# Re-planning every engine's order with other durations, other delays, other priorities and other buffer choices

## What is computed

```
x = x + full(layernorm(x))          16 heads of 8, every key seen, softmax
x = x + ffn(layernorm(x))           128 -> 512 -> 128, relu
x = x + causal_and_local(layernorm(x))   two attentions with rotary q and k: causal, then a window of 32
x = x + ffn(layernorm(x))
x = x + padded(layernorm(x))        16 heads, 2 kv heads, a window of 32 around each token
x = x + moe(layernorm(x))           8 experts, top 2: silu(y W1) * (y W2), then W3 (352 wide)
x = x + sink(layernorm(x))          8 heads of 16, window 128 and the first 4 keys
x = x + moe(layernorm(x))
```

## Time and profile before

| what | value |
|---|---|
| median of three timed runs | 2377.37 us (2376.93 to 2382.76) |
| profiled execution, span from first to last instruction | 2437.9 us (its own time is not recorded apart from the span) |
| TensorE, matmuls | 2192.9 us busy, 90% |
| TensorE, weight loads | 1242.7 us, 51% |
| VectorE | 1659.9 us, 68% |
| ScalarE | 1423.4 us, 58% |
| GpSimd | 670.1 us, 27% |
| mean granted TensorE clock | 0.978 |

### The profile page before, as it was taken

How to read it: one execution, slowest core, us unless ns; L and a number is a source line. 1 busy time by engine, 2 the same in 40 slices (tenths; PEclk the granted TensorE clock), 3 DMA queues, 4 the chain that set the end, 5 groups by cost and what they waited for, 6 DMA issues and landing times.

```text
span 2437.9 us, 62962 instructions
## 1 busy us (share of the span) xinstructions
PE 2192.9 (90%) x26266; PEld 1242.7 (51%) x26290; DVE 1659.9 (68%) x3679; ACT 1423.4 (58%) x2105; POOL 670.1 (27%) x602
## 2 busy tenths in 40 slices
PE   7888998999999989899999998998988989999887
PEld 3222232232323324424553686565787877867877
DVE  8998888786788776512754466776574858675644
ACT  1367767868787778797678755454424324344322
POOL 3400000020011102321024352422244544424553
PEclk9999999999999999999999999999999989999999
DMA  6601100211130212210231563222554745634665
GB/s 171 227 17 32 42 16 17 57 45 24 28 90 17 56 23 54 79 43 22 59 99 48 156 173 88 77 78 57 154 159 143 219 133 152 197 85 138 199 201 184
DMA packets 160746, 235.23 MB, mean 96 GB/s; under 512 B 21968, under 2 KB 81872, under 8 KB 160208
## 3 DMA queue, kind: packets, MB, share of 16 engines
q1 hardware_dynamic: 145456, 206.81, 30.6%
q0 software_dynamic: 9984, 20.73, 2.5%
q10 hardware_dynamic: 5024, 3.67, 0.6%
HBM read 156.28 MB, written 73.88 MB: 94 GB/s over the span
## 4 chain that ended last, share of the span: by engine, by line
PE 62%; DVE 14%; ACT 12%; issue 6%; another core or an unknown queue 2%; DMA 2%; POOL 1%; SPq 1%; DVEq 0%; POOLq 0%; ACTq 0%
PE PS L1182 14%; ACT PT L1344 9%; PE PS L1231 8%; PE PS L1162 8%; DVE MS L1586 7%; PE PS L1131 6%; PE PS L1248 5%; PE PS L1118 3%; PE PS L1031 2%; PE PS L992 2%; PE PS L1021 2%; PE PS L1111 2%; PE PS L1192 2%; PE PS L1042 1%
## 5 line engine op out<-in xcount | busy, mean ns | idle before, releaser
L1344 ACT ACTIVATE PT<-PS 128x1024 f32<-128x1024 f32 (+5 forms) x1200 | 1013.1, 905 | 389.7 <-PE PS L1162 368.1
L1586 DVE TENSOR_REDUCE MS<-PS 128x2 f32<-128x1024 f32 (+3 forms) x736 | 783.4, 1099 | 217.6 <-PE PS L1131 196.7
L1182 PE MATMUL PS<-PT,VA 128*9 128x512 f32 (+8 forms) x6720 | 564.4, 436 | 19.9 <-ACT PT L1344 17.8
L1162 PE MATMUL PS<-QO,KO 64*64 64x512 bf16 (+6 forms) x6240 | 424.6, 307 | 40.7 <-ACT PT L1344 31.1
L1162 PEld LDWEIGHTS PS<-QO,KO 64*64 64x64 bf16 (+2 forms) x6240 | 179.9, 106 | 286.8 <-ACT PT L1344 177.1
L1131 PE MATMUL PS<-KO,QO 61*64 61x512 bf16 (+2 forms) x3520 | 287.1, 327 | 27.3 <-DVE MS L1586 14.1
L1231 PE MATMUL PS<-SG,WB 128*128 128x128 f32 x2208 | 286.1, 282 | 10.8 <-DMA WB<-in_mW 5.0
L1231 PEld LDWEIGHTS PS<-SG,WB 128*128 128x128 f32 x2208 | 268.6, 197 | 19.4 <-issue 11.8
L1825 POOL DMA_INDIRECT scr_o<-SG,TO x184 | 182.7, 993 | 251.9 <-ACT SG L1379 226.4
L1131 PEld LDWEIGHTS PS<-KO,QO 61*64 61x64 bf16 (+1 forms) x3520 | 128.4, 105 | 230.6 <-DVE MS L1586 126.5
L1182 PEld LDWEIGHTS PS<-PT,VA 128*9 128x9 f32 (+2 forms) x6720 | 126.7, 90 | 185.1 <-issue 109.8
(11 more groups left out here) (182 smaller groups left out, 2503.7 us busy)
## 6 DMA issues: line engine op xcount, KB each, us to landing
WB<-in_mW SPq DMA_DIRECT2D x184, 384.0 KB
PT<-scr_y SPq DMA_DIRECT2D x40, 264.0 KB, 3.4
PT<-scr_o SPq DMA_DIRECT2D x16, 512.0 KB, 5.4
QO<-scr_q_full SPq DMA_DIRECT2D x32, 192.0 KB
KO<-scr_k_full SPq DMA_DIRECT2D x32, 192.0 KB
QO<-scr_q_causal SPq DMA_DIRECT2D x32, 192.0 KB
QO<-scr_q_local SPq DMA_DIRECT2D x32, 192.0 KB
QO<-scr_q_padded SPq DMA_DIRECT2D x32, 192.0 KB
```

The source lines that it names most:

```text
L1162: p = mm(pb[c:c + n, h2, at:at + tn], k[:, k0 + c:k0 + c + n], q[:, t0:t0 + tn], start=not masked, stop=True, skip_group_check=masked)
L1182: p = mm(bank[32 * h:32 * h + D + 1, c0:c0 + tn], va[0:n, :], pt[0:n, plane, at:at + tn], start=s["first"] and j == 0, stop=s["last"] and ...
L1344: e = activation(pt[0:r, 0:n, a:b], ps[0:r, 0:n, a:b], ACT.Exp, scale=s["A"].scale)
L1586: v.tensor_reduce(to, got, AX.X, ALU.max).then_inc(S["top"], 1)
```

## The change

The instructions are the same, but for six more memsets at the start. What changes is the planner and its numbers.

1. Delays: one figure for all (`HOP`, 200 ns after any step) becomes one by engine (`AFTER`).
2. Durations of nearly all steps are given anew, and those of DMAs too: for the operand loads the transfer goes from 1300 ns to 1800, 2900 or 4000 ns.
3. A product (and an `up`, a `down`) had to wait in the plan for the end of the one before it in its chain and 200 ns more; now it needs only that the other one has begun (`order`).
4. Banks are taken by the longest-free one, other buffers by the first free one; before it was the other way round. A ring `CH` of 2 is taken with each chain's bank.
5. All priorities (`LEADS`, `URGENT`, `SHORT`, `SWITCH`, `WORTH`) are other numbers.
6. All eight PSUM banks are cleared at the start, not two, and TensorE waits for all.

```diff
-HOP = 200.0
-LEADS = dict(full=(2075, -1582, 2002, -3166), ..., moe1=(4124, -3793, 2105, 1583), ..., moe2=(3151, -2635, -2559, -3240))
-SHORT = dict(pe=4316.0, act=969.0, dve=1357.0, pool=17578.0, sp=22529.0)
-SWITCH = dict(whole=165.0, quarters=123.0, columns=118.0)
-WORTH = 93219.0
+LEADS = dict(full=(12575, -313, 10581, -2099), ..., moe1=(79534, -5116, -9726, -12501), ..., moe2=(-35552, -42750, -12205, 41501))
+SHORT = dict(pe=2752, act=1132, dve=1343, pool=7914, sp=10511)
+SWITCH = 100
+WORTH = 497318
+AFTER = dict(pe=215, act=165, dve=125, pool=110, sp=60)
...
-        self.held, self.ordered = {} if held is None else held, held is not None
+        self.name, self.ordered = name, ordered
...
+    def room(self, now, besides=(), leaves=0):
+        spare = [p for p in self.parts if self.since(p) <= now and not any(i in besides for i in p)]
+        if len(spare) <= leaves:
+            return None
+        return spare[0] if self.ordered else min(spare, key=self.since)
...
         for name in names.split():
-            self.due(step.signals[name], 1, at)
+            self.due(step.signals[name], 1, at + AFTER[engine])
...
-    RA = Ring("RA", 0, [(5,), (4,), (6,), (7,)], banks)
-    RB = Ring("RB", 0, [(0, 1), (2, 3), (4, 5), (6, 7)], banks)
-    RP = Ring("RP", 0, [(6,), (7,)], banks)
+    RA = Ring("RA", 0, [(5,), (4,), (6,), (7,)], banks, False)
+    RB = Ring("RB", 0, [(i, i + 1) for i in (0, 2, 4, 6)], banks, False)
+    RP, CH = Ring("RP", 0, [(6,), (7,)], banks, False), Ring("CH", 2)
...
-                chain = dict(po=RP, fc=FC) if A.name == "full" else dict(po=RP)
+                chain = dict(po=RP, ch=CH, fc=FC) if A.name == "full" else dict(po=RP, ch=CH)
...
-                    p = add("product", [("pe", 1.667 * w + 6, "product")], dict(v=v_ready, exp=[x["exp"] for x in was], before=products[-1:]),
+                    p = add("product", [("pe", int(1.667 * w) + 17, "product")], dict(v=v_ready, exp=[x["exp"] for x in was]), order=last,
...
-                        dmas=lambda s, n=n: [("q_in%s" % s.use["qo"].i, n, 2000, 1300)])
+                        dmas=lambda s, n=n: [("q_in%s" % s.use["qo"].i, n, 1600, 4000 if not A.tiled else 2900 if A.group == 1 else 1800)])
...
-                s = add("turn_mul", [("pool", 2120, "turn_mul"), ("dve", 1150, "turn_mul2")], dict(src=ready),
+                s = add("turn_mul", [("pool", 2050, "turn_mul"), ("dve", 1430, "turn_mul2")], dict(src=ready),
...
-                s = add("turn_add", [("dve", 940, "turn_add")], dict(a=[got[g]["turn_mul"], got[g]["turn_mul2"]]),
+                s = add("turn_add", [("dve", 1120, "turn_add")], dict(a=[got[g]["turn_mul"], got[g]["turn_mul2"]]),
...
-            for i in (6, 7):
+            for i in range(8):
                 v.memset(RP[i], 0.0).then_inc(S["cleared"], 1)
```

More of the change, by code:

```diff
@@ L97, in has_all @@
     def has_all(self, now):
-        return all(s.at + HOP <= now for signals in self.needs.values() for s in signals) and all(u.i is not None for u in self.within)
+        return all(s.at <= now for s in self.awaits) and all(u.i is not None for u in self.within)
     def room(self, now):
@@ L118, in __init__ @@
         self.count, self.order, self.steps = {}, {e: [] for e in ENGINES}, []
-        self.free, self.ready, self.times = {e: 0.0 for e in ENGINES}, {e: [] for e in ENGINES}, {0.0}
+        self.free, self.ready, self.times = {e: 0 for e in ENGINES}, {e: [] for e in ENGINES}, set()
         self.banks = {}
-        self.look, self.lead, self.coming, self.mode, self.moving = {}, 0.0, {e: 0.0 for e in ENGINES}, "whole", 0.0
+        self.look, self.lead, self.coming, self.mode, self.moving = {}, 0, {e: 0 for e in ENGINES}, "whole", 0
     def given(self, name, value, at):
@@ L156, in urgency @@
             then = step.on[i + 1][0]
-            short = max(self.free[then] - now, 0.0) + self.coming[then] < SHORT[then]
+            short = max(self.free[then] - now, 0) + self.coming[then] < SHORT[then]
         stays = engine == "pe" and step.mode[0] == self.mode
-        return short, step.far + step.lead + WORTH * stays
+        return short, step.far + step.lead + WORTH * stays, -step.index
     def go(self, step, i, now):
@@ L192, in go @@
                 self.due(step.signals["dma"], 16 * n, self.moving + ns)
+        for use in step.ending:
+            use.since = max(s.at for s in use.ends)
     def run(self):
+        uses = {}
+        for i, step in enumerate(self.steps):
+            step.index, step.awaits, step.ending = i, [s for signals in step.needs.values() for s in signals] + [x.begun for x in step.order], []
+            for use in step.use.values():
+                for s in use.ends:
+                    uses.setdefault(s, []).append(use)
+        for step in self.steps:
+            for s in step.signals.values():
+                step.ending += uses.get(s, [])
         self.look_ahead()
@@ L211, in run @@
             for engine in ENGINES:
-                can = [k for k in self.ready[engine] if self.free[engine] <= now and k[2] <= now and (k[1] or k[0].room(now) is not None)]
-                if can:
-                    k = max(can, key=lambda k: self.urgency(k[0], k[1], now))
-                    self.ready[engine].remove(k)
-                    self.go(k[0], k[1], now)
+                if self.free[engine] <= now:
+                    can = [k for k in self.ready[engine] if k[2] <= now and (k[1] or k[0].room(now) is not None)]
+                    if can:
+                        k = max(can, key=lambda k: self.urgency(k[0], k[1], now))
+                        self.ready[engine].remove(k)
+                        self.go(k[0], k[1], now)
         left = [step for step in self.steps if not step.seen] + [k[0] for e in ENGINES for k in self.ready[e]]
```

256 lines of the change are left out of this document (130 added, 126 removed).

## The result

| | before | after |
|---|---|---|
| median, runs taken together on one chip | 2377.15 us (4 runs, 2374.16 to 2382.76) | 2390.44 us (4 runs, 2388.15 to 2392.25) |
| ratio after / before | | 1.005 [1.0032, 1.0068] |
| profiled execution | 2437.9 us span, later 2379.2 (below) | 2387.4 us span, own time 2389.19 |

The change makes the kernel 0.5% slower, by 13 us. The forecast was 2329 us.

What follows compares the result with a forecast made beforehand. TensorE (PE) was taken as the bound, idle for 245.0 us of a 2437.9 us span. Terms -40 - 10 + 0 + 5 + 0 - 5 = -50 us gave span 2388, times 0.9752 2329 us; 8 in 10: 2245 to 2405 us.

Steps and rivals of the forecast that it cites:

- What bounds the kernel now: the scaling: Whole kernel: idle time read in the profiled span of 2437.9 us, the result multiplied by 0.9752 at the end.
- The orders, with true durations: Last third: truer durations in the plan bring its PE idle time to the preceding 720 us's rate, -40 us (0 to -94).
- Products: PE's 592 products: one in six joins another and saves mode switches, -10 us (0 to -70).
- Delays: Handovers between engines: per-engine delays replace 200 ns and take out a cushion of 35 to 75 ns, 0 (0 to +18).
- the rival without a cushion: PE after exponentials: small ACT delays stop PE, +60 us with only 20 of the gains left, 2416 us; chance 0.21.
- Buffers: PT, QO, KO, WB, HM by the first free lose slack, so ACT's exponentials may wait, +5 us (0 to +36).
- Memsets: Start of the kernel: six more on DVE take 3 us, within 3.56 us idle before the input lands, 0 (0 to +1).
- Clock: Last third: with less PE idle time a part of the granted clock comes back, -5 us (-27 to +10).
- The signs that I listed: Profile after: less late idle time, earlier `up` matmuls, more joined products, no 5 us weight wait, exponential waits near 49 us.
- The 5 us wait for the weights: PE's 4.98 us stall for weights until 1953.0 us should go, as `sink` operand loads are priced at 4000 ns.
- Idle from 1680 us on: Last third: PE's idle time was to be under 60 us, as a sign for the main term.
- the wide mix of the first rival: Early batches' experts run beside later attentions, PE everywhere as full as from 1200 to 1440 us, 2257 us; chance 0.20.

Runs made afterwards that it cites:

- before again: The kernel before, unedited, run once more with the profiler: one execution of 2381.04 us, span 2379.2 us.
- experiment 7: Kernel after without the scatters' landing wait, measured GpSimd prices, longest-free buffers, two new sets of priorities: 2516.7 and 2535.31 us; first set on another chip 2357.48 us.
- experiment 4: Four small memsets put before each of the 64 scatters: kernel after 2434.6 us (1.0232), kernel before 2403.68 us (1.0101).
- Experiment 6: Kernel after with the scatter landing's price in the plan put back from 1500 to 2700 ns, all steps re-ordered: 2461.8 us, ratio 1.0352.
- the clean pair: Kernel after without the scatters' landing wait, with buffers taken by the first free (0.9885) and by the longest free (0.9888).
- first re-planned one: Kernel after without the scatters' landing wait, measured prices, longest-free buffers, first new set of priorities: 2516.7 us (1.0331), on another chip 2357.48 us (0.9912).
- after_again: The kernel after, unchanged, on the chip where the kernel before took 2437.29 us: 2434.7 us, ratio 0.9994.

## Why the prediction was wrong

**What bounds the kernel now: the scaling.** The step "I work in the span and multiply by 0.9752 at the end" failed first. It moved the sum itself by 1 us only; the harm is that it took the idle time of that execution for the kernel's. Its 2437.9 us are not the profiler's burden, since before again is 2381.04 us at a span of 2379.2. They are close to what the same kernel takes, 2437.29 us, on the chip of experiment 7; on which chip the first profile was taken is not on record. What that execution had and before again lacks is visible in it. Waits whose end has no cause that the profile shows, in the first profile of before:

```profile
ACT HM L1366 <- remote: 29.2, 9, 4.2
ACT SG L1379 <- remote: 17.9, 10, 3.2
...
```

All waits of this kind make 97 us there. Before again and the kernel after have none. The kernel after on the chip of experiment 7 has them too (72 us), and there its idle time in the last third is 97.0 us and not 71.8. The chain of the first profile has a share that those of before again and of the kernel after lack:

```profile
PE 62%; DVE 14%; ACT 12%; issue 6%; another core or an unknown queue 2%; DMA 2%; POOL 1%; SPq 1%; DVEq 0%; POOLq 0%; ACTq 0%
```

A single core works here, so a wait on "another core" is a sign that the execution held time that the kernel's own instructions do not explain. I had the row before me and read past it.

**The orders, with true durations (-40).** This is the step that failed, twice. First its base, 93.8 us of idle time in the last third against a rate of 7.1%. In the undisturbed run the last third has 54.3 us of 699.2, 7.8%, nearly the middle's 49.6 of 720, 6.9%. By the same rule the gain would have been 54.3 - 0.069 x 699.2 = 6 us, not 40. The loose part of the earlier trace rows was that execution's and not the kernel's. Second its premise, that the new durations are true: I held three of them against the trace, and the fourth that bears, the landing of a scatter, is near the best case. Not 40 us of idle time went, but 14.7 us came. Without the scatter's wait in both kernels, the new order is ahead, 2351.2 against 2368.6 us on one chip, 17 us. So the better order exists, at under half of the size that I gave it, and the scatters take back more than that. The prediction held that the gain could not be worked out. Yet the planner, run, ends at 2314 us before and at 2296 after, each by its own prices. That is 18 us, close to the 17 measured where no scatter waits, and a better start than the idle time of a profile.

That the wait costs 35 to 39 us in the new order and 9 in the old is shown. That the price of 1500 made the order so tight is argued. The lateness against the plan times the sensitivity of experiment 4 gives an estimate of 52 x 0.7 = 36 us in the new order and 17 x 0.4 = 7 in the old, near to what the wait costs in each. But a part of the lateness is the price of an issue, and other priorities alone could have made an order as tight. Experiment 6, which was to show it, changed everything else too.

**Products (-10).** PE's busy time fell by 6.5 us, 2175.0 to 2168.5. The fillers take 81.0 us for 88.5, which is all of it. Products did not join: in the orders that the planners give, 505 of the 592 stand alone before and 526 after. So the term is zero. Whether `short` is what sends the plan back to `scores` wasn't tested.

**Delays (0) and the rival without a cushion.** The rival ended on the right side with the wrong mechanism. Its test, PE's wait for the exponentials, is 25.8 + 11.7 = 37.5 us after and 30.5 + 15.4 = 45.9 before again; it did not double, it fell. What was too tight stood at a DMA.

**Buffers (+5)**: between 0.9885 and 0.9888 in the clean pair, so zero. **Memsets (0)**: right. They end before the first statistics need VectorE, which start at 5.82 us, against 6.08 in the earlier trace rows:

```profile
0.92 4.27 DVE L1423 MEMSET PS<- 128x512 f32 x8 [0.92 <-PEq L2092]
...
5.82 1.45 DVE L1452 BATCH_NORM_STATS2 ST<-X 128x6 f32<-128x128 f32 x7
```

**Clock (-5)**: 0.981 after, 0.982 before again. Nothing. The 0.95 to 0.96 of the earlier trace rows came with that execution; before again has 0.97 in the last third, and so has the kernel after.

**The signs that I listed.** The 5 us wait for the weights is gone, as predicted: the longest of its kind is 1.0 us, and 4.6 us in before again. The `up` matmuls moved a little to the front, 1932 records after 1680 us before, now 1818, and still none before 960. Windows of that line alone, after:

```profile
1680.00:2387.40 707.40, 227.24 (x1818) 214.25 (x1816) 0.97 0.54 162
```

Idle from 1680 us on was to be under 60 us, and is 71.8. And the row-maximum reduces fill the front as before, 340.2 + 264.6 us against 344.5 + 260.2, so the wide mix of the first rival did not come.

The fastest of all versions is the kernel after without the scatter's wait, 2351 us, 1.1% under the kernel before and 1.6% under the change, on three chips.

## What to carry to other kernels

Where an order is fixed ahead from a table of durations, check every figure that stands in a chain, DMA landings and issues first, and give a landing its usual time and not its best. Run the planner before and after, and hold its pitches against those of the trace. Before building on idle time in a profile, hold the profiled execution against the timed runs, and where its span is longer than they are, look for waits without a cause in it before scaling. And where an order came from a search, changing one price can change all of it, as in experiment 6; change the program under the fixed order, in both directions, and read the sensitivity.

## What the runs showed of the hardware that was not expected

**The same program differs by occasion, and not by one factor.** The kernel before took 2377 to 2380 us on five occasions and 2437.29 us on one, +2.5%. That one was on a chip used on no other occasion, so whether the chip or the moment makes it can't be told; it is called the slow chip here. The kernel after took 2388 to 2390 and 2434.7. The first re-planned one took 2357.48 and 2516.7, +6.8%. So the slow chip even turned the order of the kernels round. The granted clock of the kernel after is no lower there (0.982 against 0.981). The executions there show waits without a cause. The kernel after (`after_again`):

```profile
ACT SG L1402 <- remote: 16.3, 7, 3.2
...
```

And the re-planned one, where they are far longer:

```profile
ACT PT L1367 <- remote: 71.3, 7, 19.3
ACT SG L1402 <- remote: 49.4, 8, 19.4
...
```

One of the two longest, in the timeline of the re-planned kernel:

```profile
1612.99 0.96 POOL L1839 DMA_INDIRECT scr_y<-XN,SL  x1 [0.30 <-issue]
...
1616.22 0.29 PE L1185 MATMUL PS<-QO,KO 64*64 64x32 bf16 x3 [1.20 <-issue]
...
1621.26 0.34 PE L1185 MATMUL PS<-QO,KO 64*64 64x160 bf16 x1 [1.12 <-issue]
...
1632.02 1.94 ACT L1367 ACTIVATE PT<-PS 128x1024 f32<-128x1024 f32 x2 [19.34 <-remote]
```

PE issues a few small matmuls, each after more than 1 us of "issue", and ScalarE stands for 19.34 us, while GpSimd issues indirect DMAs in an unbroken run, one per 0.96 + 0.30 = 1.26 us. I took the waits of this kind of over 1 us and asked whether GpSimd was issuing an indirect DMA, or had ended one less than 1.5 us before, in the middle of each. It was so for 222 of the 226 us in this execution, for 71 of 71 us in `after_again` and for 94 of 94 us in the first profile of before. Stretches of that kind fill 39%, 55% and 49% of the time between the first and the last of these waits. That makes the indirect DMAs the suspect, and it is no more than a coincidence in time. On the other chips the same run of DMAs does no harm: the re-planned kernel has none of these waits there. Why that occasion is different stays open, and so does whether the 2351 us version wins on it, which was not run there.

**The chain of a scatter has two speeds.** Back to back, indirect DMAs issue every 1.26 us, a pair in 2.52. With the wait for the landing a pair takes 3.80 us at best and up to 5.04 in the rows shown. Over all 56 gaps of the kernel after, with the other work of GpSimd between, the mean is 5.07 us.
